# A transformer block's feed-forward way down with its 512-column matmuls issued as two of 256

## The chip, the cores and the metric

One Trainium2 chip, one of its cores. The metric is the device time of one execution in microseconds (us), lower is better. The engines are TensorE (PE, its weight loads PEld), VectorE (DVE), ScalarE (ACT), GpSimd (POOL) and SyncE (SP), which issues most DMAs.

## The reference, cut to what matters

16 sequences of 256 positions, 512 features, float32. A self-attention and a cross-attention come first; the change is in the last part.

```python
xn = _adaln(x, noise_emb, ln3_w, ln3_b)                   # (16, 256, 512)
h = jax.nn.gelu(xn @ ffn_w1.T + ffn_b1, approximate=False)  # (16, 256, 2048)
x = res + (h @ ffn_w2.T + ffn_b2)                           # (16, 256, 512)
```

`h @ ffn_w2.T` is the "way down": it contracts over 2048 hidden features.

## The kernel before

**Two stages.** The first runs both attentions for all sequences, over the first 1220 us or so. The second, the feed-forward part, takes the rest; the change lies there alone.

**Tiles of the feed-forward part.** The rows (16 x 256) are cut into NU = 8 units u of 512 rows, each UT = 4 tiles of 128. The 2048 hidden features are cut into FC = 16 chunks c of 128. For each chunk and unit the hidden values `h` are held transposed, 128 features on the partitions by 512 rows. Each float32 value is split in two float32r parts, high and low (`h_hi`, `h_lo`, `w_hi`, `w_lo`), and a product of two values is the sum of three: high by high, high by low, low by high.

**The way up.** In unit 0 it is done chunk by chunk (L1284, 12 matmuls of 512 columns, streamed as two strides of 256). In units 1 to 7 two chunks form a pair and are computed with seven products instead of eight, each of 6 matmuls of 256 columns (L1314), 42 per pair. Their factors are prepared beforehand: transposes of the next unit's rows on TensorE (L1272, in groups of four), copied out by ScalarE as `xb` (L1397), and sums and differences of weights on GpSimd.

**The way down.** A step `("down", u, c)` (L1317 on) waits for `h_lo` of its chunk and adds the chunk's share to the output of four row tiles. For each tile t it issues three matmuls: the stationary operand is a 128x128 block of `h_hi` or `h_lo`, the streamed one the 512-column row `w_h` or `w_l` of the second weight matrix, the target `ps_y[:, t, :]`, one whole PSUM bank. That is 12 matmuls a step and 8 x 16 = 128 steps (one is cut in two halves of two tiles). The weight row stays in SBUF for the whole kernel in `w_hi` and `w_lo`. Each matmul comes with its own weight load. At the last chunk of a unit VectorE adds `ps_y` to the residual (L1528) and SyncE stores it.

**What sets the order.** `hidden_order()` writes one list of steps by hand, and all five engines follow it. In a pair the order on TensorE is: products 1, 2, 5, 6 (24 matmuls), one down step, product 7 (6 matmuls), one down step, products 4 and 3 (12 matmuls), and on to the next pair. So a run of 36 up matmuls, a down step, a run of 6, a down step follow each other; where transposes are due, a group of four stands before the up products.

**Between up and down.** ScalarE copies partial sums (L1358), applies gelu (L1433, L1435, L1364) and rounds to `h_hi` (L1353); VectorE adds sums and then makes `h_lo` (L1455), which the down step waits for. There are three buffers of h, set free by `down_done`. SyncE's queue loads weights (`f_raw`), rows and residuals.

The first stage has matmuls of 256 columns as well: its query and key projections (L624) write the two halves of a bank in turn, and scores (L655, L634) do too.

Of the kernel before, what the change touches and what calls it, by code (L numbers as in the profile page):

```python
# [14 lines left out]
P = 128  # L15
# [250 lines left out]
def block_kernel(nc, x, condT, ctxT, lnT, lnb, attnT, w1T, b1, w2T, b2, cos, sin, pick, ident_in, x1, x2, out):  # L266
    B, L, D = x.shape
# [5 lines left out]
    FC = F // P  # L273
# [67 lines left out]
    with ExitStack() as whole:  # L341
# [37 lines left out]
        with ExitStack() as stage:  # L379
            def sb(name, shape, dt=F32):  # L380
                return stage.enter_context(nc.sbuf_tensor(name, shape, dt))
# [87 lines left out]
            def bank(step):  # L469
                return bank_turn[step] % NB  # L470
# [598 lines left out]
        with ExitStack() as stage:  # L1069
# [46 lines left out]
            NH = 3  # L1116
            h_sb = [sb(f"h_sb{n}", [P, U]) for n in range(2)]
            h_hi = [sb(f"h_hi{n}", [P, U], F32R) for n in range(NH)]
            h_lo = [sb(f"h_lo{n}", [P, U], F32R) for n in range(NH)]

            u_sb = [sb(f"u_sb{n}", [P, L]) for n in range(3)]
            ps_y = stage.enter_context(nc.psum_tensor("ps_y", [P, UT, 512], F32))
# [13 lines left out]
            def down_row(c):  # L1136

                return 2 * c + 1 if 2 * c + 1 < EARLY else c + EARLY // 2 if c + EARLY // 2 < 4 * KC else 2 * (c + EARLY // 2 - 4 * KC)
# [6 lines left out]
            def up_row(c):  # L1145

                if 2 * c < EARLY:
                    return w_hi[:, 2 * c, :], w_lo[:, 2 * c, :]
                buffer, n = up_place(c)
                cols = slice(n * D, (n + 1) * D)  # L1150
                return cw_hi[buffer][:, cols], cw_lo[buffer][:, cols]
# [6 lines left out]
            def factor_buffer(p):  # L1158
                return (p + 1) % 2
# [79 lines left out]
            def gelus(a):  # L1239

                if a < FC:
                    return a + 1
                p, n = divmod(a - FC, 2)
                return FC + 3 * p + 2 + n
# [8 lines left out]
            def turned(u, j, half):  # L1253

                return 2 * (PER * (u - 1) + j) + half + 1

            def hidden_tensor(eng):
                ahead = pairs_begun = 0
                for step in hidden:
                    if step[0] == "turn":  # L1260
                        u, j, half = step[1:]
                        n = turned(u, j, half)
                        ahead = n
                        if n > 1:
                            eng.wait_ge(fx_full, n - 1)
                        if u > 1:
                            eng.wait_ge(c_done, 3 * pairs_begun - 2)
                        eng.wait_ge(fx_normed, PER * (u - 1) + j + 1)
                        for c in range(2):
                            for t in range(T):  # L1270
                                k = 2 * half + c
                                ins = eng.transpose(ps_h[:, 2, c * L + t * P:c * L + (t + 1) * P], xn[:, t, k * P:(k + 1) * P], ident[:, :])  # L1272
                        ins.then_inc(fx_turned, 1)
                    elif step[0] == "up":
                        c = step[1]
                        w_h, w_l = up_row(c)
                        if 2 * c >= EARLY:
                            eng.wait_ge(f_split, 2 * c - EARLY + 1)
                        if c >= NE + 2:
                            eng.wait_ge(gelu_done, gelus(c - 2))  # L1280
                        products_of = [(w, xx, k) for k in range(KC)
                                       for w, xx in ((w_h, xx_hi), (w_l, xx_hi), (w_h, xx_lo))]
                        for j, (w, xx, k) in enumerate(products_of):
                            ins = eng.matmul(ps_h[:, c % 2, :].rearrange("p (j l) -> p j l", l=L), w[:, k * P:(k + 1) * P], xx[:, :, k, :],  # L1284
                                             start=j == 0, stop=j == len(products_of) - 1)
                        ins.then_inc(up_done, 1)
                    elif step[0] == "products":
                        p, part = step[1:]
                        u = 1 + p // PAIRS
                        r = factor_buffer(p)  # L1290
                        pairs_begun = p + 1
                        if part == 0:
                            eng.wait_ge(cw_lo_done, 3 * (p + 1))
                            if p % PAIRS == 0:
                                eng.wait_ge(fx_low_done, NX * u)

                            eng.wait_ge(gelu_done, gelus(FC + 2 * p - 4) if p >= 2 else FC - 1 + p)
                        for n in PRODUCTS[part]:
                            if n == 2 and p:
                                eng.wait_ge(c_done, 3 * p - 2)  # L1300
                            if n == 2 and ahead:
                                eng.wait_ge(fx_full, ahead)
                            if n == 5:
                                eng.wait_ge(*((c_done, 3 * p) if p else (gelu_done, FC)))
                            if n in (6, 7, 4):
                                eng.wait_ge(u_copied, 3 * p + (6, 7, 4).index(n) + 1)
                            if n == 3:
                                eng.wait_ge(c_done, 3 * p + 2)
                            w0, x0 = W_PLACE[n] * WF, X_PLACE[n]
                            x_h, x_l = xf_hi[u % 2][x0], xf_lo[u % 2][x0]  # L1310
                            for k in range(2):
                                cols = slice(w0 + k * P, w0 + (k + 1) * P)
                                for j, (w, x_) in enumerate(((cw_hi[r], x_h), (cw_lo[r], x_h), (cw_hi[r], x_l))):
                                    ins = eng.matmul(ps_h[:, bank(p, n), 0:L], w[:, cols], x_[:, k, :],  # L1314
                                                     start=n in OPENS and k == 0 and j == 0, stop=k == 1 and j == 2,
                                                     skip_group_check=True)
                            ins.then_inc(up_done, 1)  # L1317
                    elif step[0] == "down":
                        u, c, *halved = step[1:]
                        a = u * FC + c  # L1320
                        row = down_row(c)
                        w_h, w_l = w_hi[:, row, :], w_lo[:, row, :]
                        eng.wait_ge(h_lo_done, a + 1)
                        if u == 0 and 2 * c + 1 >= EARLY:
                            eng.wait_ge(f_split, 2 * c + 1 - EARLY + 1)
                        for t in range(T * halved[0], T * halved[0] + T) if halved else range(UT):
                            if u and c == 0:
                                eng.wait_ge(y_added, UT * (u - 1) + t + 1)
                            for j, (h, w) in enumerate(((h_hi[a % NH], w_h), (h_hi[a % NH], w_l), (h_lo[a % NH], w_h))):
                                ins = eng.matmul(ps_y[:, t, :], h[:, t * P:(t + 1) * P], w,  # L1330
                                                 start=c == 0 and j == 0, stop=c == FC - 1 and j == 2)
                            if c == FC - 1:
                                ins.then_inc(y_done, 1)
                        if c < FC - 1 and halved != [0]:
                            ins.then_inc(down_done, 1)
# [310 lines left out]
            with nc.Block() as block:  # L1646
                block.tensor(hidden_tensor)
                block.scalar(hidden_scalar)
                block.vector(hidden_vector)
                block.gpsimd(hidden_gpsimd)  # L1650
                block.sync(hidden_sync)
# [50 lines left out]
```

## Time and profile before

| what | value |
|---|---|
| median of 3 runs | 1906.03 us (1904.61 to 1907.36) |
| profiled execution, span from first to last instruction | 1905.8 us |
| its time by the runs' measure | not given apart; the runs lie within 1.4 us of the span |
| PE busy | 1867.6 us (98%), 13460 matmuls |
| PEld busy | 1631.1 us (86%), 13460 loads |
| DVE, ACT, POOL busy | 67%, 75%, 42% |
| mean granted clock of TensorE | 0.998 |

The profile is of one execution. Matmuls are pipelined, so the duration of one is from its start to its modelled end and reaches over the start of the next; the pace is read from starts. PE busy counts the time in which any matmul is under way. In the chain of waits each piece runs from its start to the start of what follows it.

### The profile page before, as it was taken

The page shows a single profiled execution, that of the slowest core. Times are in us where ns is not written, and L with a number is a line of the kernel's source. Part 1 is how long each engine was busy: PE and PEld are TensorE (multiplying, and loading weights), DVE is VectorE, ACT ScalarE, POOL GpSimd, SP SyncE. Part 2 cuts the span into 40 slices and gives each one's busy share as a digit, 9 for nine tenths or more (in the row PEclk, how much of TensorE's full clock was granted, in tenths as well). Part 3 has the DMA queues.
Part 4 walks back from the last instruction along what each step waited for, and adds up shares of the span by engine and source line. Part 5 has one row for each costly group of instructions (what it writes and reads, how often), then busy time and mean ns, then how long its engine had stood idle before and what let it go on. Part 6 is the DMA issues. An engine that isn't in the chain of part 4 may idle for free. (4 is left out here: it accounts for less than half of the span.)

```text
span 1905.8 us, 39347 instructions
## 1 busy us (share of the span) xinstructions
PE 1867.6 (98%) x13460; PEld 1631.1 (86%) x13460; DVE 1286.3 (67%) x2241; ACT 1429.8 (75%) x3811; POOL 803.0 (42%) x834
## 2 busy tenths in 40 slices
PE   8899999999999999999999999999999999999999
PEld 6788888888878888988988887688898998989898
DVE  5877667767776776776776776346766667666754
ACT  5788878888887898888888899655656566666654
POOL 3534333443443454454454444014535445353531
PEclk9999999999999999999999999999999999999999
DMA  6777777676686678677667778433131322323130
GB/s 217 207 208 210 212 212 204 189 208 185 187 231 207 194 223 232 199 211 220 202 207 221 204 219 208 131 111 120 58 111 56 111 78 90 99 71 108 46 99 34
DMA packets 307378, 311.51 MB, mean 163 GB/s; under 512 B 22000, under 2 KB 259952, under 8 KB 307184
## 3 DMA queue, kind: packets, MB, share of 16 engines
q1 hardware_dynamic: 306576, 308.67, 55.5%
q8 instruction: 111, 1.82, 0.4%
q14 instruction: 83, 0.68, 0.1%
q10 hardware_dynamic: 608, 0.34, 0.1%
HBM read 212.46 MB, written 92.27 MB: 160 GB/s over the span
## 5 line engine op out<-in xcount | busy, mean ns | idle before, releaser
L763 ACT ACTIVATE ps_s<-ps_s,neg_max 128x256 f32<-128x256 f32 x1024 | 461.5, 454 | 52.9 <-DVE neg_max L878 49.7
L878 DVE TENSOR_REDUCE neg_max<-ps_s 128x2 f32<-128x512 f32 x512 | 349.2, 686 | 205.1 <-PE ps_s L634 204.5
L777 ACT ACTIVATE prob<-ps_s 128x512 f32<-128x512 f32 x512 | 307.9, 602 | 90.2 <-PE ps_s L655 86.0
L959 POOL TENSOR_TENSOR rope_c<-rope_c,rope_s 128x256 f32<-128x256 f32 x128 | 98.6, 770 | 316.6 <-DVE rope_s L853 316.6
L634 PE MATMUL ps_s<-kT,qT 96*128 96x256 f32 x1024 | 218.5, 295 | 11.8 <-ACT ps_s L763 6.6
L634 PEld LDWEIGHTS ps_s<-kT,qT 96*128 96x128 f32 x1024 | 168.5, 190 | 60.3 <-ACT ps_s L763 24.3
L763 ACT ACTIVATION_READ_ACCUMULATOR ps_s<-ps_s,neg_max 128x1 f32 x1024 | 217.7, 213 | 0.0
L655 PE MATMUL ps_s<-qT,kT 112*128 112x256 f32 x1024 | 207.5, 284 | 9.8 <-ACT ps_s L763 9.0
L624 PE MATMUL ps_g<-xx_hi,w_hi 128*128 128x256 f32 x1024 | 208.9, 285 | 1.8 <-issue 1.8
L624 PE MATMUL ps_g<-xx_hi,w_lo 128*128 128x256 f32 x1024 | 206.0, 283 | 0.0
L624 PE MATMUL ps_g<-xx_lo,w_hi 128*128 128x256 f32 x1024 | 205.8, 282 | 0.0
L1330 PE MATMUL ps_y<-w_hi,h_hi 128*128 128x512 f32 x512 | 201.5, 394 | 1.2 <-DVE h_lo L1455 1.2
L1330 PE MATMUL ps_y<-w_lo,h_hi 128*128 128x512 f32 x512 | 200.7, 392 | 0.0
L1330 PE MATMUL ps_y<-w_hi,h_lo 128*128 128x512 f32 x512 | 199.3, 389 | 0.0
L655 PEld LDWEIGHTS ps_s<-qT,kT 112*128 112x128 f32 x1024 | 169.3, 190 | 31.3 <-ACT ps_s L763 11.6
L1455 DVE TENSOR_TENSOR h_lo<-h_sb,h_hi 128x512 fp32r<-128x512 f32 x128 | 111.4, 874 | 104.1 <-ACT h_hi L1353 102.7
L966 POOL TENSOR_TENSOR rot_lo<-rope_c,rot_hi 128x512 fp32r<-128x512 f32 x128 | 166.5, 1301 | 22.9 <-ACT rot_hi L739 21.9
L947 POOL TENSOR_TENSOR xx_lo<-xT,xx_hi 128x512 fp32r<-128x512 f32 x66 | 86.2, 1307 | 197.5 <-ACT xx_hi L725 197.4
L1314 PE MATMUL ps_h<-xf_hi,cw_hi 128*128 128x256 f32 x592 | 167.5, 283 | 0.0
L1314 PE MATMUL ps_h<-xf_lo,cw_hi 128*128 128x256 f32 x592 | 165.8, 280 | 0.0
L1314 PE MATMUL ps_h<-xf_hi,cw_lo 128*128 128x256 f32 x592 | 165.7, 280 | 0.0
L624 PEld LDWEIGHTS ps_g<-xx_hi,w_hi 128*128 128x128 f32 x1024 | 158.1, 191 | 2.3 <-issue 2.1
(157 smaller groups left out, 4714.2 us busy)
## 6 DMA issues: line engine op xcount, KB each, us to landing
kT<-k_turned SPq DMA_DIRECT2D x384, 128.0 KB, 3.2
qT<-q_turned SPq DMA_DIRECT2D x128, 256.0 KB, 4.0
f_raw<-in_w1T SPq DMA_DIRECT2D x124, 256.0 KB, 3.0
k_turned<-rot_hi SPq DMA_DIRECT2D x64, 256.0 KB, 3.2
k_turned<-rot_lo SPq DMA_DIRECT2D x64, 256.0 KB, 2.5
q_turned<-rot_hi SPq DMA_DIRECT2D x64, 256.0 KB, 3.7
q_turned<-rot_lo SPq DMA_DIRECT2D x64, 256.0 KB, 4.2
qT<-q_turned SPq DMA_DIRECT2D x128, 128.0 KB, 4.2
```

Of the source, the lines that this page charges most:

```text
L624: ins = eng.matmul(ps_g[:, b, s * L:(s + 1) * L], w[:, row, (T * s + t) * P:(T * s + t + 1) * P], a[:, c, :], start=c == 0 and j == 0 and ...
L634: ins = eng.matmul(ps_s[:, score_bank(step), t * L:(t + 1) * L], qT[0:ROWS, quad % NQ, j, t * P:(t + 1) * P], kT[0:ROWS, quad % NQ, j, :], ...
L655: ins = eng.matmul(ps_s[:, score_bank(step), t * L:(t + 1) * L], kT[:, quad % NQ, j, t * P:(t + 1) * P], qT[:, quad % NQ, j, :], start=Tru ...
L763: ins = eng.activation(scores[:, t * L:(t + 1) * L], scores[:, t * L:(t + 1) * L], ACT.Exp, bias=neg_max[G % 2][:, t, j:j + 1], accum_out= ...
L777: eng.activation(prob[:, n % NP, :, :].rearrange("p t l -> p (t l)"), ps_s[:, score_bank(step), :], ACT.Exp).then_inc(exp_done, 1)
L878: eng.tensor_reduce(neg_max[G % 2][:, :, j], ps_s[:, score_bank(step), :].rearrange("p (t l) -> p t l", l=L), AX.X, ALU.max, negate=True). ...
L947: eng.tensor_tensor(lo[:, ks, :], xT[:, ks, :], hi[:, ks, :].bitcast(F32), ALU.subtract).then_inc(x_low_done, 1)
L959: eng.tensor_tensor(rope_c[n % 2][:, 0, :], rope_c[n % 2][:, 0, :], rope_s[:, 0, :], ALU.subtract)
L966: eng.tensor_tensor(rot_lo[:, n % NT, :, :], rope_c[n % 2][:, :, :], rot_hi[:, n % NT, :, :].bitcast(F32), ALU.subtract).then_inc(rot_lo_d ...
L1314: ins = eng.matmul(ps_h[:, bank(p, n), 0:L], w[:, cols], x_[:, k, :], start=n in OPENS and k == 0 and j == 0, stop=k == 1 and j == 2, skip ...
L1330: ins = eng.matmul(ps_y[:, t, :], h[:, t * P:(t + 1) * P], w, start=c == 0 and j == 0, stop=c == FC - 1 and j == 2)
L1455: eng.tensor_tensor(h_lo[a % NH][:, :], h_sb[a % 2][:, :], h_hi[a % NH][:, :].bitcast(F32), ALU.subtract).then_inc(h_lo_done, 1)
```

## The change

Each product of a down step is issued twice, once for output columns 0 to 255 and once for 256 to 511. For each row tile the three products of the first half come first, then the three of the second. The streamed operand and the target are cut to the half; the stationary operand is the same and is loaded again for each matmul. The start flag, which clears the bank's accumulation state, is set at the very first matmul of the bank only. The waits stand where they stood, and the signals follow the last matmul as before.

```diff
                             if u and c == 0:
                                 eng.wait_ge(y_added, UT * (u - 1) + t + 1)
-                            for j, (h, w) in enumerate(((h_hi[a % NH], w_h), (h_hi[a % NH], w_l), (h_lo[a % NH], w_h))):
-                                ins = eng.matmul(ps_y[:, t, :], h[:, t * P:(t + 1) * P], w,
-                                                 start=c == 0 and j == 0, stop=c == FC - 1 and j == 2)
+                            for d in range(2):
+                                cols = slice(d * D // 2, (d + 1) * D // 2)
+                                for j, (h, w) in enumerate(((h_hi[a % NH], w_h), (h_hi[a % NH], w_l), (h_lo[a % NH], w_h))):
+                                    ins = eng.matmul(ps_y[:, t, cols], h[:, t * P:(t + 1) * P], w[:, cols],
+                                                     start=c == 0 and j == 0 and d == 0, stop=c == FC - 1 and j == 2, skip_group_check=True)
                             if c == FC - 1:
                                 ins.then_inc(y_done, 1)
```

## Rows read from the trace of the kernel before

**Rows 1.** Busy time by stretch (start:end, length, busy us and count by engine; clock; DMA; GB/s)

```profile
0.00:1223.80 1223.80, 1190.15 (x9304) 1026.84 (x9304) 852.36 (x1573) 1023.03 (x3034) 521.39 (x536) 1.00 0.71 204
1223.80:1300.40 76.60, 76.54 (x340) 62.32 (x340) 40.17 (x64) 41.75 (x72) 18.79 (x17) 1.00 0.47 148
1300.40:1906.00 605.60, 600.88 (x3817) 541.94 (x3816) 393.79 (x604) 364.97 (x705) 262.86 (x282) 1.00 0.27 82
```

**Rows 2.** The page's slices: granted clock in tenths, 40 slices of the span

```profile
PEclk9999999999999999999999999999999999999999
```

**Rows 3.** Groups by line on TensorE, 1300.4 us to the end

```profile
L1330 PE MATMUL ps_y<-w_hi,h_hi 128*128 128x512 f32 x456 | 179.6, 394 | 1.2 <-DVE h_lo L1455 1.2
L1314 PE MATMUL ps_h<-xf_hi,cw_hi 128*128 128x256 f32 x592 | 167.5, 283 | 0.0
L1272 PE MATMUL ps_h<-ident,v_kept 128*128 128x128 f32 x96 | 14.4, 272 | 0.0
```

**Rows 4.** Chain of waits, from 1295 us: start, us, what

```profile
1300.58 2.92 PE ps_h L1314 x24
...
1309.69 4.24 PE ps_h L1314 x36
1313.93 2.75 PE ps_y L1330 x12
...
1331.44 4.10 PE ps_h L1314 x36
1335.54 2.74 PE ps_y L1330 x12
1338.28 0.71 PE ps_h L1314 x6
```

**Rows 5.** Timeline of TensorE, end of an up run, begin of a down step

```profile
1516.50 0.28 PE L1314 MATMUL ps_h<-xf_hi,cw_lo 128*128 128x256 f32 x1
1516.51 0.19 PEld L1314 LDWEIGHTS ps_h<-xf_lo,cw_hi 128*128 128x128 f32 x1
...
1516.62 0.28 PE L1314 MATMUL ps_h<-xf_lo,cw_hi 128*128 128x256 f32 x1
...
1516.74 0.40 PE L1330 MATMUL ps_y<-w_hi,h_hi 128*128 128x512 f32 x1
...
1517.21 0.39 PE L1330 MATMUL ps_y<-w_hi,h_lo 128*128 128x512 f32 x1
...
1518.13 0.39 PE L1330 MATMUL ps_y<-w_hi,h_hi 128*128 128x512 f32 x1
...
1519.26 0.39 PE L1330 MATMUL ps_y<-w_hi,h_lo 128*128 128x512 f32 x1
```

**Rows 6.** Timeline of TensorE in an up run behind transposes

```profile
1502.90 0.28 PE L1314 MATMUL ps_h<-xf_hi,cw_hi 128*128 128x256 f32 x1
...
1503.58 0.28 PE L1314 MATMUL ps_h<-xf_hi,cw_hi 128*128 128x256 f32 x1
```

**Rows 7.** Timeline of TensorE in the attention stage, matmuls in twos

```profile
46.66 0.40 PE L624 MATMUL ps_g<-xx_hi,w_lo 128*128 128x256 f32 x2
...
47.38 0.40 PE L624 MATMUL ps_g<-xx_hi,w_lo 128*128 128x256 f32 x2
...
906.60 0.40 PE L624 MATMUL ps_g<-xx_hi,w_lo 128*128 128x256 f32 x2
...
907.55 0.28 PE L624 MATMUL ps_g<-xx_hi,w_lo 128*128 128x256 f32 x1
```

**Rows 8.** TensorE busy in two dense stretches of the attention stage

```profile
20.09:31.20 11.11, 11.10 (x93) 1.00 0.26 77
722.50:781.10 58.60, 58.60 (x501) 1.00 0.70 200
```

**Rows 9.** Chain of waits around the first wait for h_lo

```profile
1352.61 0.45 PE ps_h L1272 x4
...
1353.08 0.72 ACT xb L1397 x2
...
1354.89 0.64 ACT h_hi L1353
...
1355.56 1.73 DVE h_lo L1455
1357.29 0.04 issue
1357.33 3.06 PE ps_y L1330 x12
```

**Rows 10.** DMA queues on the page: packets, MB, share of 16 engines

```profile
q8 instruction: 111, 1.82, 0.4%
```

## The prediction

> **What bounds the kernel now.** I read the stretches first [rows 1]: the change touches only the feed-forward part, from 1223.8 us on. There TensorE is busy all the time (76.54 of 76.60 us, then 600.88 of 605.60), VectorE 65%, ScalarE 60% and GpSimd 43% of the last stretch. Its clock is granted in full (the 9s of [rows 2]), so this is the 2.4 GHz level. Then the groups [rows 3]: in all of the last stretch the down matmuls waited 1.2 us for data. Nothing but TensorE's own pace therefore sets the time here, and what the down step adds or saves shows one for one in the span.
>
> The groups' mean durations mislead: 394 ns for 512 columns and 283 ns for 256 would make two halves cost 566. They are latencies of overlapping instructions. The chain of waits gives the pace instead, since it counts start to start [rows 4]. A down step of 12 matmuls of 512 columns takes 2.75 us, 0.229 each. A run of 36 matmuls of 256 columns (the up products, same array, same kind of operands) takes 4.24 us, 0.1178 each. The same run of 36 right behind transposes takes only 4.10 us, 0.1139 each. So there are two paces of the 256-column form, and the question is which the new matmuls take.
>
> The timeline shows why 256 columns are a delicate size [rows 5]. The weight load for the next matmul starts about 0.01 us behind the start of the running one, and the next matmul starts about 0.11 us after its load. With 256 columns that is the whole pitch: loading and streaming end together. With 512 columns the load is long over before the stream ends (0.23 us). Late in a down step the pitch is 0.226 (five from 1518.13 to 1519.26); at its start it is nearer to 0.235 (two from 1516.74 to 1517.21).
>
> **The change, part by part.** (1) It removes 128 down steps of 12 matmuls of 512 columns with their 12 loads, 1536 of each, and adds 24 matmuls of 256 columns with 24 loads per step, 3072 of each. The columns streamed are the same. By the usual pace the new step takes 24 x 4.24/36 = 2.827 us against 2.75: +0.077 us, and over 128 steps **+9.8 us**. That is 6 ns for each product split, 128 x 12 of them.
>
> (2) Fast pace behind transposes. Of the 96 transposes in the last stretch [rows 3] four stand in a group, so there are 24 groups, and behind each the 256-column run goes at 0.1139. Today the 512-column step ends that state: the run of 6 after it takes 0.71 us again, as everywhere [rows 4]. I let the new down step directly behind such a run keep the fast pace: it then takes 24 x 4.10/36 = 2.733 us, 0.094 less than 2.827. Six of the 24 are cut off by a wait (part 3), which leaves 18 x 0.094 = **-1.7 us**. Its bounds are 0 (the fast pace ends with the run) and all steps fast (a rival below).
>
> (3) The recurring wait. Six times in the chain TensorE reaches a down step before h_lo is ready; the first is shown [rows 9]: transposes end, ScalarE makes xb, two gelus and h_hi, VectorE then h_lo until 1357.29, and the matmuls start at 1357.33. This chain starts at the transposes and holds no down matmul; only the run of 36 lies beside it, which doesn't change. A slower down step before the transposes shifts both ends alike, so the wait stays: 0.
>
> (4) Waits and signals. The semaphore waits stand ahead of the two loops, the increments behind the last matmul, so no wait is added, and nothing is moved past a queue. Buffers of h come free 0.08 us later per step; their users on ScalarE and VectorE are idle 35 to 40% of this stretch: 0. If that cover were gone, the late one would be h_hi, at 0.08 us per step. The start flag now clears at the first half only and the second half adds behind it; no instruction comes of it.
>
> (5) More instructions for TensorE: 1536 matmuls and as many loads. Today 3817 matmuls take 605.6 us [rows 1], 0.159 us a pair; with 1368 more it is 0.118. A sequencer that falls behind was hidden by every 0.229 us matmul and no longer is. The bounds: the attention part ran 501 matmuls in 58.60 us, 0.117 a pair [rows 8], so at least that pace is fed; 93 in 11.11 us, 0.119, come from one that is nearly all 256 columns. I cost it at 0, since these lie at the pace I assume; the upper bound is a rival.
>
> (6) Fetching instructions: queue q8 moved 1.82 MB for the whole program in 111 packets [rows 10], and the DMA share here is 0.27. Some 11% more matmuls and loads cost nothing beside that. At the end of the kernel only the last step's own 0.08 us counts.
>
> Sum: +9.8 - 1.7 = **+8.1 us**. The profiled execution's span is 1905.8 us, the median of the runs 1906.0, so the two agree and I add to the median: **1914.1 us**.
>
> A rule weighed: the traces show that the slow pair of halves costs 6 ns more than one whole and the fast pair 2 x 0.1139 = 0.228, so nearly nothing [rows 4]. The Trainium skill, page "TensorE: Matmul & The Clock Gate", section "Back-to-back issue gap", gives N/2.4 + 2.5 ns for the 2.4 GHz level; by it, as an estimate, 1536 more gaps would cost 3.8 us instead of 8.1.
>
> **The rivals.**
> A. **Everything goes fast.** What ends the fast state today may be the 512-column step; without any of them, the state lasts from one group of transposes to the next. Then 3072 x 0.1139 = 349.9 us against 128 x 2.75 = 352.0, -2.1, and the up products gain as well: 2352 of them, of which 24 x (6 + 36)/2 = 504 are fast already, so 1848 x 0.0039 = -7.2. Total -9.3: **1896.7 us**, faster. For it: the matmuls of such a run lie 0.113 apart (from 1502.90 to 1503.58 six of them) [rows 6], and it stays so to its end. Against it: in attention a run behind transposes isn't fast (eight matmuls from 906.60 to 907.55, 0.119 each, the last of [rows 7]), and the first run of 24, behind a long row of 512-column matmuls, takes 2.92 us, slow from the start [rows 4]. It decides from the point where the first down step behind transposes (about 1328 us) starts at 0.114 a matmul and hands that on.
> B. **A mix that cancels.** Fast pace in some half of the down steps: 9.8 - 64 x 0.094 = +3.8; or in the down steps alone throughout, -2.1. This is 1904 to 1910, mostly **within the noise**. The gap rule quoted above would come out here too.
> C. **The pace of the projections.** In attention, matmuls that alternate between two halves of a bank, and use w_hi and w_lo, go at 0.120: six from 46.66 to 47.38 [rows 7]. The new ones share w_hi and w_lo, as the streamed operand, and alternate only every third time. 3072 x 0.120 = 368.6 against 352.0: **+16.6, 1922.6 us**.
> D. **The sequencer becomes the bound.** The densest stretches prove 0.117 to 0.119 a pair only if nothing had been taken in ahead of them. Suppose 30 of the 501 pairs of [rows 8] had been: the true rate is then 58.60/471 = 0.1244, and once no 512-column matmul lets the sequencer catch up, both down and up products go by it: 3072 x 0.1244 = 382.2, +30.2, and 2352 x 0.0066 = +15.5, so **1952 us**. The price is from 0 to that, by how far the sequencer is ahead today. Against: the last matmuls of a run of 36 still come 0.12 apart [rows 5].
> The Trainium skill, same page, section "Wait — 56ns, not 53.3ns?", gives some 62 ns per MATMUL for a sequencer in microcode; what a load costs there it doesn't say, and with the same for it a pair would need 0.124 us, an estimate; no row here shows it.
> E. **The split isn't made** (something merges the halves): 1906. I see nothing that would.
>
> **Chances.** Forecast (1911 to 1917) 0.56; A 0.14; B 0.14; C 0.11; D 0.04; E 0.01. The range takes in the forecast, B but for its lower edge, and C: 1903 to 1924. A lies below it and D above, 0.18. A measurement of this kernel can tell about 0.2%, 3.8 us, from no change. Faster: A and a little of B, 0.16. Same: most of B and E, 0.14. Slower: 0.70.
>
> **What would show it.** Down matmuls: 1024 for each of the three forms, 256 columns, and steps of 24 in 2.83 us in the chain, 2.73 only behind transposes; the up runs still 4.24 and 4.10; PE still busy all through; six waits for h_lo in the chain, as now; the attention part unchanged to 0.5 us. I am wrong if the up runs all fall to 4.10 (A), if the step takes 2.88 (C), if steps grow longer the further they stand from a wait or idle time put down to issue shows up (D), or if ScalarE or VectorE starts to release TensorE.

## The result: slower by 0.9%, and the profile after

| | before | changed |
|---|---|---|
| median of 4 runs | 1905.32 us | 1923.68 us |
| lowest, highest | 1903.43, 1907.36 | 1921.51, 1924.33 |
| ratio | | 1.009, 95% interval 1.0078 to 1.0102 |
| profiled execution: span; its own time | 1905.8; not given | 1919.4; 1921.5 |

The ratio is worth 17 us (15 to 19). The forecast was 1914.1 us, +8, so the direction was right and the size half of what came; the range, 1903 to 1924, holds the result at its very edge.

Start with what didn't change. The busy times of the changed kernel by stretch (columns as in [rows 1]):

```profile
1223.80:1300.40 76.60, 76.60 (x508) 70.02 (x507) 38.95 (x62) 39.79 (x70) 20.11 (x18) 1.00 0.44 137
1300.40:1920.00 619.60, 614.63 (x5175) 613.24 (x5174) 389.62 (x604) 363.53 (x704) 263.24 (x280) 1.00 0.26 81
```

TensorE is still busy all through and its clock granted in full; VectorE, ScalarE and GpSimd do the same work in a longer stretch. What is new is the second column of busy time: the weight loads went from 541.94 us [rows 1] to 613.24, 99% of the stretch, so the record of some load is always open (each lasts 0.19 us, longer than the step to the next). The groups answer to [rows 3]:

```profile
L1332 PE MATMUL ps_y<-w_hi,h_hi 128*128 128x256 f32 x912 | 258.8, 284 | 1.1 <-DVE h_lo L1457 1.1
...
L1332 PEld LDWEIGHTS ps_y<-w_hi,h_hi 128*128 128x128 f32 x912 | 175.0, 192 | 2.3 <-DVE h_lo L1457 2.3
```

No new releaser, and 1.1 us of waits for h_lo where there were 1.2. The time must lie in the pace, so go to the chain, which answers to [rows 4, 9]:

```profile
1299.38 2.73 PE ps_h L1314 x24
1302.10 2.88 PE ps_y L1332 x24
...
1308.56 4.24 PE ps_h L1314 x36
...
1327.54 2.88 PE ps_y L1332 x24
1330.42 0.44 PE ps_h L1272 x4
1330.86 4.10 PE ps_h L1314 x36
1334.95 2.88 PE ps_y L1332 x24
1337.83 0.71 PE ps_h L1314 x6
...
1355.52 1.73 DVE h_lo L1457
1357.25 0.04 issue
1357.30 3.14 PE ps_y L1332 x24
```

From unit 1 on a down step takes 2.88 us, 0.120 a matmul, behind whatever run it stands (in unit 0, behind 512-column up matmuls, 2.86), where the forecast had 2.83 and, behind up runs of 4.10, 2.73. The up runs are as before, 4.24 and 4.10. The sum is about 128 x (2.88 - 2.75) = +16.6 us. The spans agree: the feed-forward part begins in the chain with this piece of the changed kernel,

```profile
1220.91 2.98 PE ps_h L1284 x12
```

and with this one of the kernel before:

```profile
1223.86 2.99 PE ps_h L1284 x12
```

1919.4 - 1220.9 = 698.5 us against 1905.8 - 1223.9 = 681.9: +16.6. (The attention stage was 3 us shorter in the one execution than in the other, which is why the spans differ by 13.6 only.) The timeline of the changed kernel, from the last up matmuls into a down step, answers to [rows 5]:

```profile
1338.26 0.28 PE L1314 MATMUL ps_h<-xf_lo,cw_hi 128*128 128x256 f32 x1
1338.26 0.19 PEld L1332 LDWEIGHTS ps_y<-w_hi,h_hi 128*128 128x128 f32 x1
...
1338.38 0.28 PE L1332 MATMUL ps_y<-w_hi,h_hi 128*128 128x256 f32 x1
1338.38 0.19 PEld L1332 LDWEIGHTS ps_y<-w_lo,h_hi 128*128 128x128 f32 x1
...
1338.50 0.28 PE L1332 MATMUL ps_y<-w_lo,h_hi 128*128 128x256 f32 x1
1338.50 0.19 PEld L1332 LDWEIGHTS ps_y<-w_hi,h_lo 128*128 128x128 f32 x1
```

A load starts with each matmul, for the next one, and the next comes 0.12 us later. Two questions are open: is it the load that the matmul waits for, or a fixed cost of each matmul; and why 0.120 here, and 0.1178 and 0.1139 in the up runs. (The 0.1139 is the mean of a run of 36 with its slower first steps; once settled, these matmuls start 0.1133 apart.)

### The profile page after: what moved, and what is told of

Its sections match the earlier page's. It is cut to its first block and busy times, and to the rows that moved or that the text cites. A ratio compares the mean times of both kernels' runs of the same rounds, so it can differ in the third digit from the quotient of the medians.

```text
span 1919.4 us, 42419 instructions
## 1 busy us (share of the span) xinstructions
PE 1882.7 (98%) x14996; PEld 1711.7 (89%) x14996; DVE 1281.8 (67%) x2241; ACT 1428.1 (74%) x3811; POOL 803.4 (42%) x834
## 3 DMA queue, kind: packets, MB, share of 16 engines
q8 instruction: 123, 2.02, 0.5%
## 5 line engine op out<-in xcount | busy, mean ns | idle before, releaser
L1332 PE MATMUL ps_y<-w_hi,h_hi 128*128 128x256 f32 x1024 | 290.4, 284 | 1.1 <-DVE h_lo L1457 1.1
L1332 PE MATMUL ps_y<-w_lo,h_hi 128*128 128x256 f32 x1024 | 289.7, 283 | 0.0
L1332 PE MATMUL ps_y<-w_hi,h_lo 128*128 128x256 f32 x1024 | 289.5, 283 | 0.0
L1332 PEld LDWEIGHTS ps_y<-w_hi,h_hi 128*128 128x128 f32 x1024 | 196.4, 192 | 2.9 <-DVE h_lo L1457 2.3
L1332 PEld LDWEIGHTS ps_y<-w_lo,h_hi 128*128 128x128 f32 x1024 | 196.4, 192 | 0.6
L1332 PEld LDWEIGHTS ps_y<-w_hi,h_lo 128*128 128x128 f32 x1024 | 196.4, 192 | 0.0
L1457 DVE TENSOR_TENSOR h_lo<-h_sb,h_hi 128x512 fp32r<-128x512 f32 x128 | 105.1, 825 | 110.1 <-ACT h_hi L1355 108.3
```

The lines of the kernel that those rows point to most:

```text
L1332: ins = eng.matmul(ps_y[:, t, cols], h[:, t * P:(t + 1) * P], w[:, cols], start=c == 0 and j == 0 and d == 0, stop=c == FC - 1 and j == 2, ...
L1457: eng.tensor_tensor(h_lo[a % NH][:, :], h_sb[a % 2][:, :], h_hi[a % NH][:, :].bitcast(F32), ALU.subtract).then_inc(h_lo_done, 1)
```

## Experiments

**Is it the load? e1, an uneven cut.**

```diff
-cols = slice(d * D // 2, (d + 1) * D // 2)
+cols = (slice(0, 3 * P), slice(3 * P, D))[d]
```

> The product is cut at column 384 instead of 256, so the number of matmuls and loads is that of the changed kernel. Theory (a matmul can't start before its own weight load, 0.113 to 0.120 us behind the start of the one before, so the pitch is the larger of load and stream): 384 columns take 0.170 to 0.176, 128 columns 0.109 to 0.120, a pair 0.28 to 0.295 against 0.240; 1536 x 0.045 = +69 us on the changed kernel, some 1990 us. Rival (each matmul costs a fixed 12 ns or so on the stream whatever its width): a pair takes 0.240 as before, 128 columns come 0.066 apart, and the time is that of the changed kernel, 1923 us.

Measured: 1991.5 us (one run), and steps of 3.40 us, a pair of 384 and 128 columns 0.284. The timeline of e1 shows what each width does:

```profile
1324.18 0.34 PE L1332 MATMUL ps_y<-w_hi,h_hi 128*128 128x384 f32 x1
1324.36 0.34 PE L1332 MATMUL ps_y<-w_lo,h_hi 128*128 128x384 f32 x1
1324.53 0.34 PE L1332 MATMUL ps_y<-w_hi,h_lo 128*128 128x384 f32 x1
1324.71 0.22 PE L1332 MATMUL ps_y<-w_hi,h_hi 128*128 128x128 f32 x1
1324.77 0.27 PE L1332 MATMUL ps_y<-w_lo,h_hi 128*128 128x128 f32 x1
1324.88 0.27 PE L1332 MATMUL ps_y<-w_hi,h_lo 128*128 128x128 f32 x1
1324.99 0.40 PE L1332 MATMUL ps_y<-w_hi,h_hi 128*128 128x384 f32 x1
1325.22 0.34 PE L1332 MATMUL ps_y<-w_lo,h_hi 128*128 128x384 f32 x1
```

384 columns come 0.175 apart. Of the narrow ones the first is followed in 0.06 us, so 128 columns can stream in that time, and then each takes 0.11. The loads of the same stretch show what holds the others back:

```profile
1324.54 0.19 PEld L1332 LDWEIGHTS ps_y<-w_hi,h_hi 128*128 128x128 f32 x1
1324.71 0.19 PEld L1332 LDWEIGHTS ps_y<-w_lo,h_hi 128*128 128x128 f32 x1
1324.82 0.19 PEld L1332 LDWEIGHTS ps_y<-w_hi,h_lo 128*128 128x128 f32 x1
1324.93 0.19 PEld L1332 LDWEIGHTS ps_y<-w_hi,h_hi 128*128 128x128 f32 x1
1325.04 0.19 PEld L1332 LDWEIGHTS ps_y<-w_lo,h_hi 128*128 128x128 f32 x1
```

In this stretch loads of 128 columns come no closer than 0.11 us. With the fixed cost of the rival the time would have been the changed kernel's; the same number of matmuls costs 68 us more, since half of them stream too little to cover their loads. That the time came out at the expected 1990 is in part luck: in three of the four row tiles of a step the first 384-column matmul behind narrow ones takes 0.23 us, 0.06 more than its like, some 21 us in all, which wasn't expected and isn't explained; the first narrow matmul of each tile takes 0.05 less than the expectation gave it, some 26 us. By the Trainium skill, page "TensorE: Matmul & The Clock Gate", section "LDWEIGHTS (loading the stationary operand)", a load takes its column count over 1.2 in ns, 107 ns for 128 columns. The 0.11 us from load to load in e1 agrees; the length of each load's own record, 0.19 us, does not.

**Is it the load? e11, narrow loads.**

```diff
-ins = eng.matmul(ps_y[:, t, cols], h[:, t * P:(t + 1) * P], w[:, cols],
+rows = slice(0, P if c == 0 else P // 2)
+ins = eng.matmul(ps_y[rows, t, cols], h[:, t * P:(t + 1) * P][:, rows], w[:, cols],
```

> The changed kernel, but from the second chunk of a unit on each load takes 64 columns of the h block instead of 128 (rows 64 to 127 of each tile get the first chunk's share alone). Streams stay 256 columns. Theory (the load is what a 256-column matmul waits for): loads take half, the pace falls from 0.120 to the stream's own, 0.107 to 0.1135: 2880 x 0.0067 to 0.013 = -19 to -37 us, 1886 to 1904 us. Rival (the 0.120 is the stream's with a fixed cost per matmul): stays at 0.120 and 1922 us.

Measured: 1896.8 us (one run), 27 us less than the changed kernel and 8 less than the kernel before. The chain of e11:

```profile
1389.10 0.68 PE ps_h L1314 x6
1389.78 2.72 PE ps_y L1333 x24
1392.50 4.08 PE ps_h L1314 x36
1396.58 2.88 PE ps_y L1333 x24
1399.45 0.70 PE ps_h L1314 x6
1400.16 2.73 PE ps_y L1333 x24
1402.89 4.08 PE ps_h L1314 x36
1406.97 2.72 PE ps_y L1333 x24
```

As many matmuls of 256 columns, 24 a step, now 0.1133 apart. So the 0.120 isn't a price of issuing a matmul; it goes when the load takes half as many columns. The chain holds its own control: the step of 2.88 at 1396.58 is the first of a unit, the one kind that e11 leaves with full loads, and among half-loaded neighbours, right behind a run of 4.08, it is back at 0.120. (A load of 64 columns also means that 64 output partitions are written instead of 128; no run tells the two apart, so that it is the load is argued with the help of e1.) What I hadn't foreseen is that the up runs, whose own loads still have 128 columns, fall to 4.08 us and 0.68 us as well, and that the run of 6 behind the full step is slow again, 0.70. So an up run takes its pace over from what stands before it, with the same operands; a down step with full loads does not.

**How does the cost grow? d1, two tiles of four.**

```diff
-for d in range(2):
-    cols = slice(d * D // 2, (d + 1) * D // 2)
+for d in range(2 if t < 2 else 1):
+    cols = slice(d * D // 2, (d + 1) * D // 2) if t < 2 else slice(0, D)
```

> Halves for row tiles 0 and 1 of each step only, whole products of 512 for tiles 2 and 3 (for the step cut in two, the same by tile). Theory: twelve matmuls at 0.120 and six at 0.229 or so, 1.44 + 1.39 = 2.83 us a step, +0.08 x 128 = +9 to +10 us on the kernel before, 1915 us; half the effect. Rival (the cost comes with the change of form, whatever its amount): nearer to the full +17, 1922 us; or (no 512-column matmul any more matters) nearly nothing until all are split.

Measured: 1915.5 us, ratio 1.0052 (1.0037 to 1.0067), and in its chain

```profile
1306.57 2.83 PE ps_y L1332 x18
1309.39 4.24 PE ps_h L1314 x36
```

Somewhat over half of the effect (10 us of 17), 0.08 a step as expected: the cost grows with the number of products that are split, roughly in proportion, and the remaining wholes take their 0.23.

**Which order of operands? e2, e3, e4.** e2 puts the two halves of a product side by side, so that the bank's halves alternate at each matmul and a block is loaded twice in a row:

```diff
-for d in range(2):
-    for j, (h, w) in enumerate(...):
+for j, (h, w) in enumerate(...):
+    for d in range(2):
```

> The two halves of one product stand side by side, so each block of h is loaded twice in a row and the target half changes at every matmul instead of every third. Theory (load bound, and 0.120 is the load's turnaround): pace 0.120, time as the changed kernel within 0.3%, 1923 us. Rival 1 (changing the half of the bank costs): three times as many changes, so slower than 0.120; at 6 ns a change 2048 more changes are +12 us, 1935. Rival 2 (a block loaded again is cheaper): pace toward 0.113 for half of the matmuls, 1923 - 10 = 1913 us.

Measured: 1921.6 us, ratio 1.0084 (1.0069 to 1.0099); steps of 2.88. Both rivals of its expectation fall. e3 changes the order of the three terms in the up products of the kernel before:

```diff
-enumerate(((cw_hi[r], x_h), (cw_lo[r], x_h), (cw_hi[r], x_l)))
+enumerate(((cw_hi[r], x_h), (cw_hi[r], x_l), (cw_lo[r], x_h)))
```

> The kernel before, with the three terms of each up product in the order of the down step (high x high, high x low, low x high, the stationary operand first), so that the stationary block repeats and the streamed one changes at each matmul. Down step of 512 columns as before. If the order of operands sets the difference between 0.1178 (up) and 0.120 (down halves), the up runs of 36 go from 4.24 to 4.32 us and the kernel gains 2352 x 0.0022 = 5 us, 1910 us. If the order is indifferent (the pace belongs to the tensors or their places), the up runs stay at 4.24 and the time at 1905 us.

Measured: 1905.5 us, ratio 0.9999 (0.9990 to 1.0009); runs of 4.24 and 4.10 as before. e4 does the reverse in the changed kernel's down step:

```diff
-((h_hi[a % NH], w_h), (h_hi[a % NH], w_l), (h_lo[a % NH], w_h))
+((h_hi[a % NH], w_h), (h_lo[a % NH], w_h), (h_hi[a % NH], w_l))
```

> The changed kernel, with the three terms of each half in the order of the up products, so that the streamed block repeats and the stationary one alternates. If the order sets the pace, the down step goes from 2.88 to 2.83 us or to the fast 2.73: 128 x 0.05 = -6 us, 1917, or down to 1904 us. If it doesn't, 2.88 and 1923 us.

Measured: 1922.2 us, ratio 1.0090 (1.0073 to 1.0107); steps of 2.88. These orders make no difference.

**Which place? e5, e6, e7.** Each takes one place out of the changed kernel's down step.

```diff
-ins = eng.matmul(ps_y[:, t, cols], h[:, t * P:(t + 1) * P], w[:, cols],
+ins = eng.matmul(ps_y[:, t, cols if c == 0 else slice(0, D // 2)], h[:, t * P:(t + 1) * P], w[:, cols],   # e5
+ins = eng.matmul(ps_y[:, t, cols], h[:, t * P:(t + 1) * P], w[:, 0:D // 2],   # e6
+ins = eng.matmul(ps_y[:, t, cols], h[:, 0:P], w[:, cols],   # e7
```

> The changed kernel, but from the second chunk of a unit on both halves are added into output columns 0 to 255 (columns 256 to 511 get the first chunk's share alone). The up products, at 0.1178, write one half of their bank too. If writing both halves of a bank makes the down pace 0.120, the down step falls from 2.88 to 2.83 us or 2.73, 1923 to 1917 or less. If the pace is the load's and doesn't depend on the target: 2.88 and 1923 us.

> The changed kernel, but both halves stream columns 0 to 255 of the weight row (the second half of w2 is left out, the output's second half repeats the first). If the places that are streamed set the pace (two 1 KB parts of a row in turn): 2.83 us a step or less, 1917 or less. If not: 2.88 and 1923 us.

> The changed kernel, but all four row tiles use the h block of the first (the hidden values of tiles 1 to 3 are left out of the way down), so the loads read two places all the time. If the place of the load sets its turnaround: 2.83 us a step or less, 1917 or less. If not: 2.88 and 1923 us.

Measured, one run each: 1921.5, 1922.8 and 1925.1 us. The steps in the traces decide rather than these single times: 2.88 in all three. Neither the half that is written, nor the half that is streamed, nor the block that is loaded makes the 0.120.

**Alignment? e9 and e10.** By the sizes of the buffers that the kernel places ahead of it, `w_hi` should begin 32 bytes behind a multiple of 64 in its partition, and the other operands with it; no trace shows addresses. One line shifts them in the changed kernel (e9) and in the kernel before (e10):

```diff
+keep("pad", [P, 8])
 w_hi, w_lo = (keep(f"w_{part}", [P, 4 * KC, D], F32R) for part in ("hi", "lo"))
```

> The changed kernel with 32 bytes per partition left free ahead of w_hi, so that every operand of the feed-forward matmuls moves from 32 bytes behind a multiple of 64 to a multiple of 64. If the alignment of loads and streams makes the turnaround 0.120: the down step goes from 2.88 to 2.73 us, 128 x 0.15 = -19 us, 1903, the up runs to 4.10. If the turnaround doesn't hang on it: 2.88, 4.24 and 1922 us.

> The kernel before with the same 32 bytes. If alignment decides: up runs 4.24 to 4.10 (-8 us) and the attention stage's 256-column matmuls faster too, 1895 us or less. If not: 1905 us.

Measured: e9 1921.4 us, ratio 1.0085 (1.0072 to 1.0099), steps of 2.88; e10 1904.6 us, ratio 0.9996 (0.9987 to 1.0004), runs of 4.24 and 4.10. A shift by 32 bytes changes nothing.

**Can the up runs be pushed to the pace of 0.1139? e8.** In e1 every up run stood behind 128-column matmuls and most took 4.16 us. e8 therefore cuts the first matmul of each run of 36 in the kernel before:

```diff
+cut = 2 if n == 4 and k == 0 and j == 0 else 1
+for s in range(cut):
+    part_ = slice(s * L // cut, (s + 1) * L // cut)
-    ins = eng.matmul(ps_h[:, bank(p, n), 0:L], w[:, cols], x_[:, k, :],
+    ins = eng.matmul(ps_h[:, bank(p, n), part_], w[:, cols], x_[:, k, part_],
```

> The kernel before (down steps of 512 columns), with the first matmul of each up run of 36 split in two of 128 columns, same result. In the uneven split, every up run behind a 128-column matmul came down to 0.1133 a matmul after five or six, where it stays at 0.1178 behind a 512-column one. Theory (the pace of 256 columns depends on how load and stream stand to each other when a run begins, and lasts until another width comes): the runs of 36 take 4.14 us or so instead of 4.24 with the split's own 0.06 included, 50 runs x 0.1 = -5 us, 1900 us. Rival (the state comes from what stood before the run, the split inside it does nothing): +0.06 x 56 = +3 us, 1909 us.

Measured: 1906.0 us, ratio 1.0007 (0.9998 to 1.0016). Its chain:

```profile
1306.26 4.22 PE ps_h L1317 x37
1310.48 2.74 PE ps_y L1333 x12
...
1327.52 0.44 PE ps_h L1272 x4
1327.96 4.35 PE ps_h L1317 x37
```

The run of 36 (37 with the cut) gets 0.02 us shorter, not 0.10: the narrow pair and the matmuls next to it take nearly all that the rest gains. Behind transposes, where the run was fast (4.10), the cut makes it 4.35. By the starts in e8's timeline the pace did change: the cut run behind a down step settles at 0.1133 after some eight matmuls, and the cut run behind transposes, at 0.1133 without the cut, settles at 0.1178. So what stands at the head of an up run changes its pace. But the expectation was wrong in size, and nothing is won.

## Why the prediction was right, and where its size was off

**What bounds the kernel: right.** TensorE's pace set the time, one for one; the 16.6 us of the down steps are all of it, and no wait was added.

**Part 1, the usual pace: the step that was mis-sized.** I priced the halves by the up runs, 4.24/36 = 0.1178 [rows 4], for they stand in the same stretch and write one half of a bank as the new ones do for three matmuls. They took 0.120, the pace of the projections [rows 7], rival C, which I gave 0.11. The term was +9.8; with 2.88 a step it is +16.6, that is 6.8 more. Of two paces of one form in the trace I took the one nearest in time, and nothing that I had read excluded the other. That the result lies in the range is owed to rival C's having been taken into it; the forecast's own sum came to half of the effect. That much is luck.

**Part 2, the fast pace behind transposes: wrong.** It was to give 1.7 us back. The trace shows 2.88 directly behind a run at 4.10 (1330.86, then 1334.95). Even the run of 6 behind transposes lost it, 0.71 for 0.70. With part 1 this closes the sum: 8.1 + 6.8 + 1.7 = 16.6.

**Part 3, the recurring wait: right in its cause.** Six waits for h_lo in the chain, as before, released in the same way by the chain from the transposes (1.73 us of h_lo, then 0.04); the step behind one takes 3.14 against 3.06 [rows 9].

**Parts 4 to 6: right.** No release by ScalarE or VectorE, queue q8 at 2.02 MB and 123 packets for 1.82 MB and 111 [rows 10] without a trace in the time.

**The rule weighed.** The 2.5 ns a gap of the Trainium skill's page "TensorE: Matmul & The Clock Gate" ("Back-to-back issue gap") would, as an estimate, have given 3.8 us for the change; measured are 0.240 - 0.229 = 11 ns a split product, four times that. The runs show that a term for the stream alone can't do at this width: with the loads halved in e11 the pace falls from 0.120 to 0.1133.

**The rivals.** A (everything fast) didn't come about; with lighter loads, in e11, nearly all down steps and up runs go at 0.1133, and the time is 1896.8 against the 1896.7 of A, though for a computation that loads half. B and D have nothing for them: no down step of the changed kernel settles at the fast pace, and e11 issues as many matmuls and loads as the changed kernel at 0.1133 a pair, so 0.120 is not the sequencer's limit. C had the right number (1922.6 us) for a partly wrong reason: it named the alternating halves and the tensors w_hi and w_lo. e2 and e5 exclude the halves of the bank; the streamed half (e6) and the loaded block (e7) don't matter either, nor does the order (e3, e4).

**Open.** Why a run of 256-column matmuls settles at 0.1133, 0.1178 or 0.120. Shown is that the down steps with halved loads went at 0.1133 and those with full loads at 0.120 in one and the same run (e11), that the pace of an up run hangs on its forerunner and its head, and that order, target, streamed half, loaded block and a shift by 32 bytes leave the 0.120 alone. The time of a full load by itself isn't the answer: such loads came every 0.11 us in e1, and its up runs, with full loads, settled at 0.1133. So full loads are one condition of the 0.120, and something in the down step that these runs don't name is another. Whether the tensors themselves decide, say by h against cw as the loaded operand, wasn't tried.

## What to carry to other kernels

A matmul that streams 256 columns takes about as long (0.1133 us with light loads) as the load of the next 128-column block (0.11 from load to load), so neither hides the other; 512 columns hide the load, and 128 cost 0.11 us instead of 0.06. Before you split a streamed operand, ask whether each piece still covers a load, and price it by all paces that the trace shows for that width, not by the nearest. The duration of a matmul in a table (283 ns here) says nothing of its cost; starts do (120 ns).

## What was not expected of the hardware

- A 256-column stream has several stable paces, 0.1133, 0.1178 and 0.120 us a matmul, each held to the end of a run. The pace of an up run depends on its forerunner: with the same operands the runs of 36 took 4.24 us behind 512-column steps and behind full 256-column ones, 4.16 behind 128-column matmuls (e1; 0.1133 once settled) and 4.08 behind steps with 64-column loads (e11).
- In the changed kernel a run of 24 up matmuls behind 512-column ones took 2.73 us (the first line of the chain above), where the same run took 2.92 before [rows 4].
- In e1 a first 384-column matmul behind three of 128 took 0.23 us to the next start, 0.06 more than its like.
